# Edge blocks gathered in groups of eight, four and two, and dense products issued in two runs of twelve matmuls per pass

## The reference, cut to what matters

```
u = xn @ root + bias
for r in range(R):
    mask = (edge_type == r)
    sums = segment_sum(xn[src] * mask[:, None], dst, n)
    cnt  = segment_sum(mask, dst, n)
    u = u + (sums / maximum(cnt, 1)[:, None]) @ weight[r]
z = concatenate([u, xn], 1) @ w_gate + b_gate
h = tanh(u) * z + xn * (1 - z)            # then x = x + h
# after that: top-2 of 8 experts, two products each, layer norm, residual
```

## Time and profile before

| | us |
|---|---|
| median of three runs | 2188.13 (2180.44 to 2189.11) |
| the profiled execution, its own time | 2187.53 |
| its span | 2185.7 |
| gather stage within the span, first block's matmuls to last flush | 967 to 1567 |
| PE busy over the span | 2011.1 (92%) |
| DVE busy | 1284.4 (59%) |
| ACT busy | 969.2 (44%) |
| mean granted TensorE clock | 0.956 |

### The profile page before, as it was taken

How to read it: one execution, slowest core, us unless ns; L and a number is a source line. 1 busy time by engine, 2 the same in 40 slices (tenths; PEclk the granted TensorE clock), 3 DMA queues, 4 the chain that set the end, 5 groups by cost and what they waited for, 6 DMA issues and landing times. The chain is left out here.

```text
span 2185.7 us, 28064 instructions
## 1 busy us (share of the span) xinstructions
PE 2011.1 (92%) x9425; PEld 1596.2 (73%) x9425; DVE 1284.4 (59%) x2282; ACT 969.2 (44%) x1506; POOL 904.0 (41%) x801
## 2 busy tenths in 40 slices
PE   8999999999999999999899899899799579899970
PEld 6777778778888888877677577677488468788860
DVE  8589588832222222139899899899798742222215
ACT  3211122222222222249899799899644223233332
POOL 0000046565655555237677588688200022212212
PEclk9999999999999999999899899999799779999995
DMA  5224487777777877679889799899565579998439
GB/s 185 100 81 134 137 272 247 259 251 253 254 258 259 256 258 256 227 223 321 273 292 315 242 329 319 272 331 313 194 178 176 199 266 326 305 318 287 103 75 188
DMA packets 156848, 520.96 MB, mean 238 GB/s; under 512 B 30748, under 2 KB 31132, under 8 KB 154672
## 3 DMA queue, kind: packets, MB, share of 16 engines
q1 hardware_dynamic: 85616, 310.51, 41.1%
q0 software_dynamic: 71104, 208.84, 32.1%
HBM read 383.83 MB, written 154.68 MB: 246 GB/s over the span
## 5 line engine op out<-in xcount | busy, mean ns | idle before, releaser
L211 PE MATMUL psum<-w_hi,xnT_hi 128*128 128x512 f32 (+1 forms) x1592 | 421.1, 399 | 4.6 <-PEq L228 2.5
L211 PE MATMUL psum<-w_lo,xnT_hi 128*128 128x512 f32 (+1 forms) x1592 | 417.8, 393 | 0.0
L211 PE MATMUL psum<-w_hi,xnT_lo 128*128 128x512 f32 (+1 forms) x1592 | 413.7, 394 | 0.0
L882 POOL DMA_INDIRECT sorted_rows<-acc x313 | 342.9, 1096 | 116.7 <-issue 85.3
L580 ACT ACTIVATE work<-psum 128x512 f32<-128x512 f32 (+1 forms) x150 | 89.7, 598 | 661.5 <-PE psum L211 661.5
L211 PEld LDWEIGHTS psum<-w_hi,xnT_hi 128*128 128x128 f32 (+1 forms) x1592 | 293.5, 187 | 75.4 <-issue 4.0
L211 PEld LDWEIGHTS psum<-w_lo,xnT_hi 128*128 128x128 f32 (+1 forms) x1592 | 294.9, 185 | 73.2
L211 PEld LDWEIGHTS psum<-w_hi,xnT_lo 128*128 128x128 f32 (+1 forms) x1592 | 294.3, 185 | 71.1
L982 POOL DMA_INDIRECT w_hi<-y_rows,sort_row x168 | 221.2, 1317 | 78.3 <-PE psum L1115 41.3
L982 POOL DMA_INDIRECT w_lo<-y_rows,sort_row x164 | 217.9, 1329 | 77.2 <-PE psum L1115 38.6
L1108 PE MATMUL psum<-y_hi,hot 128*128 128x512 f32 x664 | 220.0, 414 | 30.2 <-ACT y_hi L1030 27.4
(11 more groups left out here) (334 smaller groups left out, 2614.0 us busy)
## 6 DMA issues: line engine op xcount, KB each, us to landing
split_experts<-acc SPq DMA_DIRECT2D x128, 512.0 KB, 4.2
ring<-split_experts SPq DMA_DIRECT2D x16, 4096.0 KB, 16.1
w_raw<-in_wchunks SPq DMA_DIRECT2D x86, 512.0 KB, 5.0
y_rows<-work SPq DMA_DIRECT2D x144, 256.0 KB, 2.8
acc<-in_wchunks SPq DMA_DIRECT2D x64, 512.0 KB, 6.0
work<-local_rows SPq DMA_DIRECT2D x26, 384.0 KB, 4.2
sum_rows<-work SPq DMA_DIRECT2D x22, 256.0 KB, 4.5
acc<-in_bias SPq DMA_DIRECT2D x10, 512.0 KB, 5.5
```

The source lines that it names most:

```text
L211: i = pe.matmul(to[:rm, :], x_[:, k, m * P:m * P + rm], w_[:, s, k * HALF:(k + 1) * HALF], start=(n == 0), stop=(n == 3 * KD - 1))
L882: pool.indirect_dma_start(sorted_dram, IndirectOffsetOnAxis(ap=e_dest[:, c:c + 1], axis=0), e_rec[:, c, :], None, bounds_check=BLOCKS * P ...
```

## The change

It alters three things in the gather stage and the sorting code that feeds them.

- Groups: 34 groups of eight blocks (a whole pass, summed in one pair of PSUM banks), 10 of four and 10 of two. There are still 332 blocks and 44 passes; flushes fall from 88 to 54. `starts` is split into `starts`, `shifts` and `owners`, and `positions` gets a second threshold and shift for each tile (two more DVE operations) and is done one tile per step.
- Which passes are short: passes 5, 11, 22, 33 and 43 have groups of two (four blocks); 4, 10, 21, 32 and 39 two groups of four; all others one group of eight. So the passes with weight pieces now have eight blocks, with pieces 0 and 1 before the second block, piece 2 before the seventh and piece 3 before the eighth. Passes 5, 11, 22 and 33 carry a unit beside their four blocks.
- The unit: twelve matmuls after the blocks of the first half of a pass and twelve after those of the second, none within a block.

The diff, cut to its core (`starts` and its two new parts are mostly left out):

```diff
--- before.py
+++ after.py
@@ -23,11 +23,12 @@
 EC = -(-EDGES // EP)
 PAD_DST = P * 4096
 GROUP = 4
-SHORT = GROUP // 2
-SHORT_GROUPS = TILES
-LONG_GROUPS = -(-((EDGES + TILES * (SHORT * P - 1)) // (SHORT * P) - SHORT_GROUPS) // 4) * 2
-GROUPS = LONG_GROUPS + SHORT_GROUPS
-BLOCKS = LONG_GROUPS * GROUP + SHORT_GROUPS * SHORT
+LONG, SHORT = 2 * GROUP, GROUP // 2
+SIDE_GROUPS = 2 * TILES
+LONG_GROUPS = -(-((EDGES + TILES * (SHORT * P - 1)) // (SHORT * P) - 3 * TILES) // 4)
+GROUPS = LONG_GROUPS + SIDE_GROUPS
+BLOCKS = LONG_GROUPS * LONG + TILES * GROUP + TILES * SHORT
+QUADS = 2 * LONG_GROUPS + SIDE_GROUPS
...
-PASSES = GROUPS // 2
+PASSES = QUADS // 2
...
+        e_last = e_count[:, 0:EC]
...
+                def shifts():
+                    v.tensor_tensor(mid_used, t_mid_start[:, TILES - 1:TILES], t_mid[:, TILES - 1:TILES], ALU.add)
...
+                def owners():
+                    side = slice(LONG_GROUPS, GROUPS)
...
                     for t in range(1, TILES):
-                        v.scalar_tensor_tensor(out=short_tile, in0=short_f, scalar=t_odd_start[:, t:t + 1], in1=short_tile,
+                        v.scalar_tensor_tensor(out=mid_tile, in0=side_mid, scalar=t_mid_start[:, t:t + 1], in1=mid_tile,
+                                               op0=ALU.is_ge, op1=ALU.add)
+                        v.scalar_tensor_tensor(out=odd_tile, in0=side_odd, scalar=t_odd_start[:, t:t + 1], in1=odd_tile,
                                                op0=ALU.is_ge, op1=ALU.add)
                         link(v.scalar_tensor_tensor(out=l_tile, in0=group_f, scalar=t_start[:, t:t + 1], in1=l_tile,
...
                 def positions(first, last):
                     for t in range(first, last):
                         link(v.tensor_scalar(e_mask, e_tile, float(t), None, ALU.is_equal))
                         link(v.tensor_tensor_scan(e_scan, e_ones, e_mask, 0.0, ALU.mult, ALU.add))
-                        link(v.tensor_scalar(e_tail, e_scan, t_tail[:, t:t + 1], t_shift[:, t:t + 1], ALU.is_gt, ALU.mult))
+                        v.tensor_scalar(e_tail, e_scan, t_mid_at[:, t:t + 1], t_mid_shift[:, t:t + 1], ALU.is_gt, ALU.mult)
+                        link(v.tensor_scalar(e_last, e_scan, t_odd_at[:, t:t + 1], t_odd_shift[:, t:t + 1], ALU.is_gt, ALU.mult))
                         link(v.tensor_tensor(e_scan, e_scan, e_tail, ALU.add))
+                        link(v.tensor_tensor(e_scan, e_scan, e_last, ALU.add))
                         link(v.scalar_tensor_tensor(out=e_scan, in0=e_scan, scalar=t_off[:, t:t + 1], in1=e_mask,
                                                     op0=ALU.add, op1=ALU.mult))
                         link(v.tensor_tensor(e_pos, e_pos, e_scan, ALU.add))
...
-                side = {(HIST_CHUNK, 3): [turned], (HIST_CHUNK, 5): [starts],
-                        (HIST_CHUNK + 1, 2): [lambda: positions(0, 3)], (HIST_CHUNK + 1, 6): [lambda: positions(3, 6)],
-                        (HIST_CHUNK + 2, 0): [lambda: positions(6, 8)], (HIST_CHUNK + 2, 2): [lambda: positions(8, TILES)],
-                        (HIST_CHUNK + 2, 4): [records], (LOOK_CHUNK, 0): [table]}
+                side = {(HIST_CHUNK, 3): [turned], (HIST_CHUNK, 5): [starts], (HIST_CHUNK, 8): [shifts],
+                        (HIST_CHUNK + 2, 4): [records], (HIST_CHUNK + 2, 8): [owners], (LOOK_CHUNK, 0): [table]}
+                for t in range(TILES):
...
-        SHORT_PASSES = (*PIECES_AT, PASSES - 1)
-        ORDER, FIRST, COLUMN = [], [0], []
+        SHORT_PASSES = (*(i + 3 for i in PIECES_AT if i + 3 < PASSES), TILES // 2, PASSES - 1)
+        MID_PASSES = (*(i - 1 for i in SHORT_PASSES[:-1]), PASSES - 5)
+        assert not {*SHORT_PASSES, *MID_PASSES} & {*PIECES_AT}
+        KIND = [SHORT if i in SHORT_PASSES else GROUP if i in MID_PASSES else LONG for i in range(PASSES)]
+        BASE = {LONG: 0, GROUP: LONG_GROUPS * LONG, SHORT: LONG_GROUPS * LONG + TILES * GROUP}
+        NUMBER = {LONG: 0, GROUP: LONG_GROUPS, SHORT: LONG_GROUPS + TILES}
+        taken = {kind: 0 for kind in BASE}
+        OWNER, BEGINS, ENDS, PAIR, FIRST, COLUMN, pair = [], [], [], [], [0], [], -1
         for i in range(PASSES):
             for h in range(2):
-                short = i in SHORT_PASSES
-                n = sum((g >= LONG_GROUPS) == short for g in ORDER)
-                at, size = (LONG_GROUPS * GROUP + n * SHORT, SHORT) if short else (n * GROUP, GROUP)
-                ORDER.append(LONG_GROUPS + n if short else n)
-                COLUMN += range(at, at + size)
+                kind = KIND[i]
+                begins, ends = kind < LONG or h == 0, kind < LONG or h == 1
+                n, part = taken[kind], h * GROUP if kind == LONG else 0
+                pair += begins
+                OWNER.append(NUMBER[kind] + n)
+                BEGINS.append(begins)
+                ENDS.append(ends)
+                PAIR.append(pair)
+                at = BASE[kind] + n * kind + part
+                COLUMN += range(at, at + min(kind, GROUP))
                 FIRST.append(len(COLUMN))
+                taken[kind] += ends
         assert sorted(COLUMN) == list(range(BLOCKS))
 
         def size_of(g):
 
             return FIRST[g + 1] - FIRST[g]
 
-        def pieces_in(i):
-
-            return [(PIECES_AT[i], q) for q in range(PIECES)] if i in PIECES_AT else []
+        PIECES_BEFORE = {1: (0, 1), 6: (2,), 7: (3,)}
+
+        def pieces_in(i, n=None):
+
+            if i not in PIECES_AT:
+                return []
+            return [(PIECES_AT[i], q) for q in (range(PIECES) if n is None else PIECES_BEFORE.get(n, ()))]
...
-                        if pieces:
-                            c, q = pieces[n]
+                        for c, q in pieces_in(i, n):
...
-                    tile = v.value_load(group_tile[0:1, ORDER[g]:ORDER[g] + 1], min_val=0, max_val=TILES - 1)
-                    accumulate(ACC_NO[g], acc[:, bass.ds(tile, 1), :].rearrange("p o n -> p (o n)"),
-                               psum[:, 2 * (g % 2):2 * (g % 2) + 2, :].rearrange("p b n -> p (b n)"))
+                    tile = v.value_load(group_tile[0:1, OWNER[g]:OWNER[g] + 1], min_val=0, max_val=TILES - 1)
+                    two = 2 * (PAIR[g] % 2)
+                    accumulate(ACC_NO[PAIR[g]], acc[:, bass.ds(tile, 1), :].rearrange("p o n -> p (o n)"),
+                               psum[:, two:two + 2, :].rearrange("p b n -> p (b n)"))
...
-                            if pieces:
-                                lo_piece(v, pieces[j - FIRST[2 * i]][0], 0, pieces[j - FIRST[2 * i]][1])
+                            for c, q in pieces_in(i, j - FIRST[2 * i]):
+                                lo_piece(v, c, 0, q)
...
-                        if g >= 1:
+                        if g >= 1 and ENDS[g - 1]:
...
-                        if g >= 2:
-                            pe.wait_ge(acc_done, ACC_NO[g - 2])
+                        if BEGINS[g] and PAIR[g] >= 2:
+                            pe.wait_ge(acc_done, ACC_NO[PAIR[g] - 2])
+                        two = 2 * (PAIR[g] % 2)
                         pe.wait_ge(hot_done, g + 1)
                         for j in range(FIRST[g], FIRST[g + 1]):
                             b, k = j % SLOTS, j - FIRST[g]
-                            first, last = k == 0, k == size_of(g) - 1
+                            first, last = BEGINS[g] and k == 0, ENDS[g] and k == size_of(g) - 1
                             pe.wait_ge(hi_done, j + 1)
                             for q in range(2):
-                                o = pe.matmul(bank[2 * h + q], hot[:, h, k, :], y_hi[:, j % 2, q * HALF:(q + 1) * HALF],
+                                o = pe.matmul(bank[two + q], hot[:, h, k, :], y_hi[:, j % 2, q * HALF:(q + 1) * HALF],
                                               start=first, stop=False)
                             o.then_inc(hi_used, 1)
-                            for _ in itertools.islice(steps, 3 * KD // SLOTS):
-                                pass
                             pe.wait_ge(lo_done, j + 1)
                             for q in range(2):
-                                o = pe.matmul(bank[2 * h + q], hot[:, h, k, :], slot_of(b)[:, q * HALF:(q + 1) * HALF],
+                                o = pe.matmul(bank[two + q], hot[:, h, k, :], slot_of(b)[:, q * HALF:(q + 1) * HALF],
                                               start=False, stop=last)
                             o.then_inc(pe_done, 1)
+                        for _ in itertools.islice(steps, 3 * KD // 2):
+                            pass
...
```

More of the change, by code:

```diff
@@ L416, in program @@
         group_i, group_f, l_tile = carve(GROUPS, I32), carve(GROUPS), carve(GROUPS)
[L417 to L420, removed]
+        t_bit = carve(TILES, I32)
+        t_mid, t_odd, t_mid_start, t_odd_start = (carve(TILES) for _ in range(4))
+        t_mid_at, t_mid_shift, t_odd_at, t_odd_shift = (carve(TILES) for _ in range(4))
```

(36 more changed lines are left out.)

45 lines of the change are left out of this document (27 added, 18 removed).

## The result

The changed kernel takes 2293.04 us (median of five, 2289.83 to 2298.49) against 2188.13 for the kernel before; the ratio is 1.0484, 95% interval 1.0464 to 1.0504. The profiled execution has a span of 2288.1 us, 102.4 us more than before. The forecast was 2294.5 us, with a range of 2230 to 2345. One of the seven executions of the first experiment took 2580.3 us at a mean granted clock of 0.738 where the others have 0.96; its median holds it (2178.5 us without), the ratios don't.

A forecast was written before the change was run, and what follows sets the result against it. It took PE's idle time to bound the kernel. Runs of twelve cost 40 + 63 + 5 us, short and piece passes gained 6, sorting cost 5: 107 us on 2187.53, so 2294.5 us, range 2230 to 2345.

The forecast's parts named there:

- What bounds the kernel: Whole kernel: PE, busy 92% of the span, sets the pace; the change is worth what it does to PE's idle time.
- The flushes: Gather stage: 88 become 54, 41 us less on DVE, of which at most 2.4 us could be seen.
- The two runs of twelve: Full gather passes: PE waits after each run; passes take 15.6 or 16.9 us, losing 40, 63 and 5 us; bounds 81 to 135.
- with a copy: Gather passes where ACT first copies the previous unit (20 to 39): 16.9 us, 3.95 us lost in each of 16, 63 us.
- Short passes and pieces: Gather stage: short passes with a unit 41 us, piece passes 68 plus 8 for the clock; 117 against 123, 6 us gained.
- Sorting: Sorting code: longer positions on DVE make PE's count matmuls wait some 5 us around chunk 3; bounds 0 and 8.
- DVE's lag and lead: Sorting: DVE loses 1.7 us per step through ten steps, 15 to 17 us, having begun about 10 us ahead.
- The sum: All terms: 40 + 63 + 5 - 6 + 5 = 107 us slower on the profiled 2187.53, giving 2294.5 us.
- The supply didn't keep up: Rival for the gather stage: ACT and DVE bridge the runs, 10 to 20 us faster, 2168 to 2178 us; chance 0.12.
- that rival's condition: Gather half pass: y_hi 3 would have to start 0.85 us sooner, before the run ends, in a third buffer.
- The clock didn't fall in plain passes: Rival for the gather stage: every run of twelve made at 1.2 GHz, 210 us more, 2505 us; chance 0.03.

The follow-up runs named there:

- the first experiment: Changed kernel with the unit's matmuls put back between high and low part of each block: 2179.89 us, ratio 0.9932 to the kernel before; measured again 2181.07 us, 0.9958.
- experiment 5: Kernel before, groups of four and two kept, with only the unit moved to twelve matmuls after each half pass: 2304.07 us, ratio 1.0528.
- experiment 7: The first experiment with every group of eight summed and added to acc as two halves, so 88 flushes and not 54: 2184.02 us, ratio 0.9987.
- experiment 1: The same run as the first experiment: changed kernel with the unit's matmuls back between high and low part of each block, 2179.89 us, ratio 0.9932.
- (2): Changed kernel, runs of twelve kept, with a third y_hi buffer and one buffer instead of two for the copied unit: 2242.04 us, ratio 1.0224.
- (6): Changed kernel with the unit in four runs of six per pass, one after every second block: 2215.92 us, ratio 1.0128.
- 3: Changed kernel with ACT's copy of units 20 to 39 moved from before the second block of the next pass to before the third: 2272.03 us, ratio 1.0363.

## Why the prediction was right

**What bounds the kernel** was read rightly: PE's idle time, not DVE's busy time, decides. The flushes fell as computed, 54, and 41 us less of DVE gave no time in the changed kernel (experiment 5, with 88 flushes, has the same passes of 15.8 and 17.1 us); experiment 7 puts their worth at 3 to 12 us once PE is fed, where the prediction allowed 2.4. It had the passes at 13.1 and 12.95 us from matmuls counted in windows of 15 us; they are 13.4 and 13.15 long, and with fewer flushes the first are 13.0 (experiment 1), so 0.4 us a pass could be won and not 0.15.

**The two runs of twelve.** 7.8 us for a half pass, 7.93 measured; 15.6 for a pass, 15.8 measured; 16.9 with a copy, 17.1 measured. Against passes of 13.4 and 13.15 us that makes 16 x 2.4 + 16 x 3.95, 38 + 63 us, where 40 + 63 were forecast. Both pass lengths, before and after, were 0.2 to 0.3 us too short in the forecast, and the differences came out right by that, which is luck for this part of the number. The mechanism is shown from four sides: undone (1), done alone (5), with the missing buffer given (2) and with shorter runs (6); the part of the copy is shown by 3.

**Short passes and pieces.** The piece passes came out as forecast: 71.7 us before (71 forecast) and 77.3 after (76 forecast). The clock is at 0.50 for 27 us of the gather stage, where it was for 65 before, so it fell there as forecast, though for less time than before. The four short passes with a unit take 39.9 us (41 forecast) against 53.1 for the full ones that were at their places (52). What was mis-sized stands behind the piece passes: with them, passes 9, 20, 31 and 42 took 126.1 us before and 132.8 after, so these four lost 1.1 us. The forecast had let 9, 20 and 31 lose 7.7 us (2.5 + 2.6 + 2.6) like any other full pass. Pass 31 did (12.5 to 14.6 us), but 9 and 20 were 14.7 and 14.8 us long before and are 14.6 and 13.9 now. Why wasn't traced.

**Sorting** is the step that failed in its detail, though its size was inside the bounds. "So PE's count matmuls wait some 5 us in all around chunk 3": PE waited 5.0 us, but not there. The first thing in DVE's queue that came too late for PE was the last weight piece, without which chunk 3 can't start; DVE's lag and lead, 15 and 10 us in the forecast, weren't measured by themselves. And since it came as one wait and not in small parts, the clock fell to 0.50 and took 2.2 us more: 7.4 us, within the bound of 8. The stage starts 9.1 us later since 1.9 us come on top in chunks 7 to 15, for which the forecast had no term.

**The sum.** 107 us were forecast and 102.4 came between the two profiled executions, 104.9 between the medians: 93.5 in the gather stage (102 forecast) and 9.1 before it (5). Of the 8 us missing in the stage, 6.6 are those of the passes behind the piece passes; the rest is made of differences of 1 to 2 us in several terms. Half of that error was made good by the 4 us that the sorting cost over its forecast, and that is luck.

**The rivals.** The supply didn't keep up, and it is the buffer that decides: with a third one, as that rival's condition said, y_hi 3 is ready and passes fall to 13.1 to 14.0 us. With PE fed, the regrouping gains 22 us of the stage (experiment 1), within the 10 to 26 that this rival gave to pieces and short passes plus 2.4 for the flushes. The clock didn't fall in plain passes; it is at 1.00 in all of them. These rows speak for short gaps only: the waits in plain passes are under 2 us, and behind the one of 5.0 us in the sorting the clock was at 0.50.

## What to carry to other kernels

Independent matmuls placed between the two halves of a dependent step do double work: they are progress, and they are the time in which other engines prepare the next step. Gathered into a run, they leave the other engines idle as soon as the buffers are full, and afterwards only the prepared steps are there to cover the supply of the next. So compare two times: how long the main engine has work once the run is over, and how long it takes until the next step is ready, here 3.15 us by the prediction's working. Two blocks are 1.86 us of work, 1.3 us too little in each half, and passes were 15.8 us. Three blocks are 2.8 us, and two blocks with a run of six behind them 3.3; these are estimates of the same kind, and passes were 13.1 to 14.0 and 13.2 us. Look also at what the supplying engine does in order, such as the copy that waits for the end of the run. An engine relieved of 41 us of work gave back 3 to 12 us, those of the passes in which it was the last to be ready; and where a full engine's queue gets longer, the wait comes at the first result needed behind it.

## What the runs showed of the hardware that was not expected

A single wait of PE of 5.0 us put it 7.4 us behind, as the clock stood at 0.50 (1.2 GHz) until about 5 us after the restart, while the waits in plain passes, 1.3 us or more in every 7.9 us and some 100 us in sum, cost no clock at all. The mean clock of the slower kernel is the higher one, 0.964 against 0.956: in its gather stage 27 us passed at 0.50, where it had been 65. And the same 240 dense matmuls take 55.67 us in all kernels with the new groups and 55.45 in the two without them, for a reason that no run here shows.
